# A gated Mamba2 layer with a small expert network on one Trainium2 core: the expert stage in another order

## Chip, core and metric

The kernel runs on one NeuronCore of one Trainium2 chip. The metric is device time in microseconds (us) of one execution. The kernel before takes 1638.48 us, the median of 3 runs (1638.3 to 1638.57).

## What is computed

The input is x, 1024 tokens (4 sequences of 256) of 512 channels in float32. Everything works on its layer norm xn, and the result is `x + s * silu(e)`, where s is a Mamba2 layer and e a small mixture of experts:

```
proj = xn @ in_proj_w.T                       # gate 8192, x 8192, B and C 8 x 128 each, dt 128
xBC  = silu(causal convolution of 4 taps)
dt   = clip(softplus(dt + dt_bias), 0.001, 100)
y    = chunked scan (chunks of 128, 128 heads of 64) + x * D
s    = grouped RMS norm(y * silu(gate)) * norm_w @ out_proj_w.T

probs     = softmax(xn @ gate_w.T)            # 16 experts
vals, idx = top_k(probs, 2);  vals /= sum(vals)
w[token, idx] = vals                          # 0 elsewhere
h = silu(xn @ g.T) * (xn @ u.T)               # 16 experts x 56 channels = 896
e = sum over experts of (h * w) @ d
```

## The kernel before

All products keep float32 accuracy by splitting both operands into a high part (rounded to the float32r type) and a low part (the rest). `product` (lines 448 to 451) then issues three matmuls: high x high, high x low of the tokens, low x high of the weights. A **block** (`channels`) is one tile of 128 output channels over 512 tokens: four contraction tiles of three matmuls, 12 in all.

The program has a prelude and then a long loop. The loop goes over 8 groups of 16 heads, in two halves of 512 tokens each, in 8 steps per half. It isn't touched by the change. The **prelude** normalizes and transposes the tokens, computes the experts, the routing and the time steps, and leads into the loop. It takes about the first tenth of the time.

The experts are computed in 14 tiles e = 0 to 13: 7 tiles of 128 of the 896 channels for each half of the tokens. Tile e = (half, f) needs:

- `expert_in(half, f, 0)` and `expert_in(half, f, 1)` on PE, a block each, for gate and up. Its weights come in through 4 slots of `stg` on SP's DMA queue. ACT writes the high part (`split_first`, line 777), and GpSimd (POOL) the low part (`split_lo`, line 1014), which then frees the slot for SP's next load.
- `expert_tanh(e)` on ACT (line 783) and `expert_gated(e)` on DVE (lines 1118 and 1127), which also free the PSUM banks for tile e + 2.
- `expert_weights(half, f)` on PE (lines 522 and 523): two matmuls that copy each token's routing weight to the 128 channels of the tile, into the PSUM bank `tb`. There is one such bank, so tile e + 1 waits until `expert_weighted(e)` on DVE (line 1133) has read it.
- `expert_hi(e)` on ACT and `expert_lo(e)` on DVE: the split of the result, in 7 buffers for a half. `experts_out(half, t)` on PE needs all 7; it is 21 matmuls for each of the 4 token tiles of a half.

The routing runs across engines: `router` (24 matmuls on PE), `router_turn` (transposes, line 482), `router_exponents` and `router_weights` on DVE, and `route` (transposes on PE, line 564). ACT and DVE then split the weights (lines 843 and 1237), and only then can `expert_weights(0, 0)` run. In `router_weights` 16 small instructions (line 1181), two for each of the 8 token tiles, compare the expert numbers 0 to 15 with a token's chosen index and multiply by its weight. The time steps run between them: `steps_in`, `steps_turn` (line 499), a softplus on ACT (lines 833 to 837) and four wide instructions on DVE (lines 1220 to 1232), `cumulate` and `cumulate_turn`.

At the very start DVE computes mean and variance of 8 token tiles (`tile_stats`), POOL raises the variance to the power -0.5 (`deviation`, line 1009), DVE normalizes (line 1106), PE transposes (`turn_tile`, line 466), ACT and DVE split the transposed tile (lines 764 and 1112). Token tiles 0 to 3 are the first half.

Each engine executes its instructions in the order in which they are written in its own section, and waits on semaphores. No scheduler moves anything: the order of the work is the order of these calls.

Of the kernel before, what the change touches and what calls it, by code (L numbers as in the profile page):

```python
# [7 lines left out]
ALU = mybir.AluOpType  # L8
# [5 lines left out]
P = 128  # L14
# [6 lines left out]
NTT = T // P  # L21
# [132 lines left out]
def build(nc, hid, wstream, wdt, cparams, dtb, rw, consts, sel, out):  # L154
    with ExitStack() as ctx:
# [288 lines left out]
        def _(pe):  # L444
# [138 lines left out]
            steps_turn()  # L583
            experts_in(0, 3)
            experts_in(0, 4)
            experts_in(0, 5)
            route()
            expert_in(0, 6, 0)
            expert_weights(0, 0)
            expert_in(0, 6, 1)  # L590
            expert_weights(0, 1)

            for f in range(3):
                expert_in(1, f, 0)
                expert_weights(*divmod(2 * f + 2, NF))
                if f == 1:
                    cumulate_turn()
                expert_in(1, f, 1)
                expert_weights(*divmod(2 * f + 3, NF))
                if f == 0:  # L600
                    cumulate()
            experts_out(0, 0)
            expert_in(1, 3, 0)
            expert_weights(1, 1)
            expert_in(1, 3, 1)
            expert_weights(1, 2)
            experts_out(0, 1)
            experts_in(1, 4)
            expert_weights(1, 3)
            experts_out(0, 2)  # L610
            experts_in(1, 5)
            expert_weights(1, 4)
            experts_out(0, 3)
            experts_in(1, 6)
            expert_weights(1, 5)
            expert_weights(1, 6)
# [113 lines left out]
            for s in range(4, NJ):  # L730
                step(-1, 1, s, False)
                experts_out(1, s - 4)
# [25 lines left out]
        def _(act):  # L758
# [53 lines left out]
            expert_tanh(0)  # L812
            turned(7)
            for p in FSTEP[0]:
# [3 lines left out]
            expert_tanh(1)  # L818
# [3 lines left out]
            for p in FSTEP[1]:  # L822
                split_first(FPOS[p])
# [5 lines left out]
            expert(2)  # L829
            expert(3)  # L830
# [6 lines left out]
            nc.scalar.activation(tmp1, tmp2, ACT.Ln, bias=1.0).then_inc(S["sp_l"], 1)  # L837
            expert(4)
            expert(5)
            act.wait_ge(S["rt_T"], 1)  # L840
            for i in range(2):
                src = (tb[0:NE, :], pr[2][0:NE, :])[i]
                nc.scalar.activation(wT_hi[i], src, ACT.Copy).then_inc(S["rt_hi"], 1)
            expert(6)
            expert_hi(0)
            expert_hi(1)
            expert(7)
            for i in range(3):
# [6 lines left out]
            expert_hi(2)  # L855
            expert_hi(3)
            expert(8)
            expert_hi(4)
            expert_hi(5)
            expert_tanh(9)  # L860
            expert_hi(6)
            for p in FSTEP[9]:
                split_first(FPOS[p])
            out_tanh(0)
            expert(10)
            out_tanh(1)
            expert(11)
            out_tanh(2)
            expert(12)
            for e in range(7, 11):  # L870
                expert_hi(e)
            out_tanh(3)
            expert(13)
            for e in range(11, 14):
                expert_hi(e)
# [126 lines left out]
        def _(pool):  # L1002
# [88 lines left out]
        def _(dve):  # L1091
# [71 lines left out]
            def router_weights():  # L1163
# [15 lines left out]
                for i in range(NTT):  # L1179
# [359 lines left out]
```

## Time and profile before

| | before |
|---|---|
| median of 3 runs | 1638.48 us |
| profiled execution: its own time | 1638.45 us |
| profiled execution: span | 1636.3 us |
| PE busy | 1598.9 us (98%) |
| DVE busy | 1411.6 us (86%) |
| ACT busy | 1198.4 us (73%) |
| POOL busy | 957.9 us (59%) |
| DMA, mean over the span | 132 GB/s |

The span is the time between the first and the last recorded instruction; the profiled execution's own time is 2.15 us longer. The chain of work that ended last is 84% PE, 8% DVE, 3% ACT and 1% POOL. A row of the timeline gives an instruction's start and its length. An "idle before" beside it is the time for which the engine stood still, with the instruction that released it. Matmuls are pipelined and their ends are modelled: in a full stream the starts lie closer together than the lengths.

### The profile page before, as it was taken

The numbers are of one execution on the slowest core, as the hardware profiler recorded it, in microseconds if no ns is written. First come the engines' busy times: TensorE is split into PE (matmuls) and PEld (weight loads), VectorE is DVE, ScalarE is ACT, GpSimd is POOL, SyncE is SP. The second block draws the span as 40 slices with busy tenths as digits, with TensorE's granted clock in tenths as the row PEclk, the third lists the DMA queues.
The fourth block names the chain that finished last, engine by engine and source line by source line (L and its number), as shares of the span: only waits on it lengthen the run. The fifth ranks groups of instructions, "written<-read, shape, count | busy, mean of one in ns | idle before, by whom it ended". The sixth has DMA issues, their size and how long they took to land.

```text
span 1636.3 us, 28479 instructions
## 1 busy us (share of the span) xinstructions
PE 1598.9 (98%) x8484; PEld 1269.6 (78%) x8484; DVE 1411.6 (86%) x1664; ACT 1198.4 (73%) x2305; POOL 957.9 (59%) x593
## 2 busy tenths in 40 slices
PE   7899989999999999999999999999999999999998
PEld 5677867877778777787777777877778778778776
DVE  6553699988998899998898899989898899889987
ACT  3432688778787778878787878778787878778782
POOL 4522266666566556666566656665576655666563
PEclk9999999999999999999999999999999999999999
DMA  4322344434343344433443334443343434334432
GB/s 150 94 98 94 115 143 149 148 106 150 131 145 135 122 148 147 143 112 123 151 156 128 119 131 152 140 131 129 138 158 110 137 130 158 134 114 148 155 129 90
DMA packets 83719, 216.48 MB, mean 132 GB/s; under 512 B 10576, under 2 KB 12880, under 8 KB 83424
## 3 DMA queue, kind: packets, MB, share of 16 engines
q1 hardware_dynamic: 83264, 214.15, 38.9%
q8 instruction: 81, 1.33, 0.3%
q14 instruction: 86, 0.70, 0.1%
q10 hardware_dynamic: 288, 0.30, 0.1%
HBM read 209.43 MB, written 4.98 MB: 131 GB/s over the span
## 4 chain that ended last, share of the span: by engine, by line
PE 84%; DVE 8%; issue 3%; ACT 3%; POOL 1%; DMA 0%; ACTq 0%; DVEq 0%; POOLq 0%; SPq 0%
PE pj L449 15%; PE pj L451 14%; PE pj L450 14%; PE pr L449 8%; PE pr L450 7%; PE pr L451 7%; PE sc L661 7%; PE sc L665 3%; PE tb L650 3%; DVE conv L1309 2%; POOL w_lo L1014 1%; DVE wo_lo L1373 1%; ACT decay L915 1%; PE pr L639 1%; DVE xc L1323 1%
## 5 line engine op out<-in xcount | busy, mean ns | idle before, releaser
L1014 POOL TENSOR_TENSOR w_lo<-stg,w_hi 128x512 fp32r<-128x512 f32 x316 | 496.2, 1571 | 348.7 <-ACT w_hi L889 263.8
L449 PE MATMUL pj<-xT_hi,w_hi 128*128 128x512 f32 x1208 | 479.3, 397 | 15.8 <-POOL w_lo L1014 7.2
L451 PE MATMUL pj<-xT_hi,w_lo 128*128 128x512 f32 x1208 | 472.6, 391 | 0.0
L450 PE MATMUL pj<-xT_lo,w_hi 128*128 128x512 f32 x1208 | 472.4, 391 | 0.0
L1309 DVE SCALAR_TENSOR_TENSOR conv<-pj,par,conv 128x510 f32<-128x510 f32 (+2 forms) x480 | 357.7, 745 | 80.5 <-ACT conv L897 67.1
L915 ACT ACTIVATE decay<-decay,dtg 128x256 f32<-128x256 f32 (+1 forms) x1024 | 379.0, 442 | 0.0
L1048 POOL TENSOR_TENSOR xc<-xc,thg 128x512 f32<-128x512 f32 x128 | 203.1, 1587 | 188.1 <-DVE xc L1360 188.0
L1054 POOL TENSOR_TENSOR sqsum<-sqsum,sq 128x512 f32<-128x512 f32 x112 | 218.1, 1947 | 114.5 <-ACT sq L941 111.0
L449 PEld LDWEIGHTS pj<-xT_hi,w_hi 128*128 128x128 f32 x1208 | 227.8, 189 | 73.2 <-issue 14.2
L451 PEld LDWEIGHTS pj<-xT_hi,w_lo 128*128 128x128 f32 x1208 | 227.9, 189 | 48.5
L450 PEld LDWEIGHTS pj<-xT_lo,w_hi 128*128 128x128 f32 x1208 | 228.1, 189 | 45.4
L1337 DVE TENSOR_TENSOR decay<-decay,gm 128x1536 f32<-128x1536 f32 x128 | 242.0, 1890 | 0.0
L904 ACT ACTIVATE thx<-conv 128x512 f32<-128x512 f32 x160 | 101.2, 633 | 175.9 <-DVE conv L1309 175.9
L449 PE MATMUL pr<-wo_hi,yT_hi 128*128 128x512 f32 x540 | 221.6, 410 | 0.0
L450 PE MATMUL pr<-wo_lo,yT_hi 128*128 128x512 f32 x540 | 211.1, 391 | 0.0
L451 PE MATMUL pr<-wo_hi,yT_lo 128*128 128x512 f32 x540 | 210.3, 389 | 0.0
L1323 DVE SCALAR_TENSOR_TENSOR xc<-thx,conv 128x512 f32<-128x512 f32 x128 | 196.8, 1542 | 0.2
L923 ACT ACTIVATE decay<-decay 128x1536 f32<-128x1536 f32 x128 | 189.2, 1478 | 0.1
L889 ACT ACTIVATE w_hi<-stg 128x512 fp32r<-128x512 f32 x285 | 176.3, 619 | 17.3 <-PE pj L451 14.5
L661 PE MATMUL sc<-decay,xdt 128*64 128x256 f32 x1024 | 160.5, 392 | 0.0
L897 ACT ACTIVATE conv<-pj,par 128x512 f32<-128x512 f32 x160 | 123.4, 771 | 26.4 <-PE pj L451 25.8
L928 ACT ACTIVATE thg<-pj 128x512 f32<-128x512 f32 x128 | 75.2, 588 | 91.1 <-PE pj L451 91.1
(178 smaller groups left out, 1995.0 us busy)
## 6 DMA issues: line engine op xcount, KB each, us to landing
stg<-wstream SPq DMA_DIRECT2D x387, 256.0 KB, 2.7
decay<-cs_scr SPq DMA_DIRECT2D x128, 768.0 KB, 4.3
acc<-hid SPq DMA_DIRECT2D x8, 256.0 KB, 4.8
out<-acc SPq DMA_DIRECT2D x8, 256.0 KB, 2.0
dt_scr<-decay SPq DMA_DIRECT2D x1, 1024.0 KB, 4.9
gate_scr<-part SPq DMA_DIRECT2D x4, 256.0 KB, 2.0
dtg<-dt_scr SPq DMA_DIRECT2D x16, 64.0 KB, 4.2
stg<-hid SPq DMA_DIRECT2D x4, 256.0 KB, 4.9
```

The source lines that it names most:

```text
L449: nc.tensor.matmul(dst, hi_w, hi_x, start=first, stop=False)
L450: nc.tensor.matmul(dst, hi_w, lo_x, start=False, stop=False)
L451: return nc.tensor.matmul(dst, lo_w, hi_x, start=False, stop=last)
L661: nc.tensor.matmul(sc[hd, c0:c0 + 2 * P], xdt[:, j % 2, 2 * b, hd], decay[:, j % NDEC, 2 * h + b, 0:2 * P], start=True, stop=False)
L915: ins = nc.scalar.activation(d, d, ACT.Relu, scale=-1.0, bias=dtg[:, half, 1, 2 * b + late, 2 * n + h:2 * n + h + 1])
L923: nc.scalar.activation(d, d, ACT.Exp, scale=-1.0).then_inc(S["exp"], 1)
L1014: nc.gpsimd.tensor_tensor(w_dest(n, 1), stg[:, s % RING, :], f32(w_dest(n, 0)), ALU.subtract).then_inc(S["wl"], 1)
L1048: nc.gpsimd.tensor_tensor(xc[:, j, :], xc[:, j, :], thg[:, j % 2, :], ALU.mult).then_inc(S["yg"], 1)
L1054: nc.gpsimd.tensor_tensor(sqsum[:, :], sqsum[:, :], sq[:, :], ALU.add).then_inc(S["sa"], 1)
L1309: nc.vector.scalar_tensor_tensor(out=y[:, :, n:], in0=x[:, :, 0:256 - n], scalar=par[:, 5 * m + 3 - n:5 * m + 4 - n], in1=y[:, :, n:], op0 ...
L1323: nc.vector.scalar_tensor_tensor(out=dst, in0=thx[:, m % 2, :], scalar=1.0, in1=conv[:, m % 2, :], op0=ALU.add, op1=ALU.mult).then_inc(S[" ...
L1337: nc.vector.tensor_tensor(d, d, gm[:, half].unsqueeze(1).to_broadcast([P, 2, 2, 3 * P]), ALU.mult).then_inc(S["w"], 1)
```

## The change

The change is to the order of calls in the prelude, on four engines, and to the instructions of one computation. SP's section is untouched.

- **POOL**: the deviations of token tiles 4 to 7 come after the low parts of the first four weight tiles, not before and between them.
- **PE**: three blocks run ahead of the transposes of token tiles 4 to 6, where one did. Two more blocks run ahead of the time steps (`steps_in`), and one more ahead of `steps_turn`. `route` runs right after `steps_turn` (it was after tile 5), and `expert_weights(0, 0)` two tiles sooner. From there each tile's weighting follows at every block, and `experts_out(0, t)` stand ahead of tiles (1, 2) to (1, 5). `expert_weights(1, 6)` stands between the first two blocks of the next stage.
- **ACT and DVE**: their calls follow the same order. The split of the routing weights stands ahead of the softplus on ACT, and right behind the two additions of the bias on DVE.
- **`router_weights`**: the 16 compare-and-multiply instructions of 128 x 16 become two comparisons and two multiplications of 128 x 128, over all token tiles at once, with broadcast operands.

```diff
 # PE
-            expert_in(0, 0, 0)
+            expert_in(0, 0, 0)
+            expert_in(0, 0, 1)
+            expert_in(0, 1, 0)
             turn_tile(4)
             turn_tile(5)
             turn_tile(6)
-            expert_in(0, 0, 1)
+            expert_in(0, 1, 1)
             turn_tile(7)
-            expert_in(0, 1, 0)
+            expert_in(0, 2, 0)
             router()
-            expert_in(0, 1, 1)
+            expert_in(0, 2, 1)
             router_turn()
             steps_in()
-            experts_in(0, 2)
+            expert_in(0, 3, 0)
             steps_turn()
-            experts_in(0, 3)
-            experts_in(0, 4)
-            experts_in(0, 5)
             route()
+            expert_in(0, 3, 1)
+            expert_in(0, 4, 0)
+            expert_weights(0, 0)
+            expert_in(0, 4, 1)
+            expert_weights(0, 1)
...
+            expert_in(1, 0, 0)
+            expert_weights(0, 6)
+            cumulate()
+            expert_in(1, 0, 1)
+            expert_in(1, 1, 0)
+            expert_weights(1, 0)
+            cumulate_turn()
+            expert_in(1, 1, 1)
+            for f in range(2, 6):
+                experts_out(0, f - 2)
                 expert_in(1, f, 0)
+                expert_weights(1, f - 1)
                 expert_in(1, f, 1)
+            expert_in(1, 6, 0)
             expert_weights(1, 5)
-            expert_weights(1, 6)
+            expert_in(1, 6, 1)
...
-            for s in range(4, NJ):
+            channel_block(-1, 1, ("x", 0))
+            expert_weights(1, 6)
+            channel_block(-1, 1, ("x", 1))
+            experts_out(1, 0)
+            for s in range(5, NJ):
 # ACT
+            expert_tanh(0)
+            for p in FSTEP[0]:
+                split_first(FPOS[p])
+            expert_tanh(1)
             turned(4)
             turned(5)
             turned(6)
...
-            expert(2)
-            expert(3)
+            expert_tanh(3)
+            split_first(FPOS[FSTEP[3][0]])
+            act.wait_ge(S["rt_T"], 1)
+            for i in range(2):
+                src = (tb[0:NE, :], pr[2][0:NE, :])[i]
+                nc.scalar.activation(wT_hi[i], src, ACT.Copy).then_inc(S["rt_hi"], 1)
 # POOL
-            for i in range(5):
+            for i in range(4):
                 deviation(i)
             n = 0
             for s, (kind, half, i) in enumerate(FSEQ):
-                if 1 <= s <= 3:
-                    deviation(4 + s)
+                if s == RING:
+                    for t in range(4, NTT):
+                        deviation(t)
 # DVE, router_weights
-                for i in range(NTT):
-                    for j, dst in enumerate((wr, wr1)):
-                        nc.vector.tensor_scalar(dst[:, i, :], iota, ixf[:, i, j:j + 1], w2[:, i, j:j + 1],
-                                                ALU.is_equal, ALU.mult).then_inc(S["rt_x"], 1)
-                dve.wait_ge(S["rt_x"], 44)
+                for j, dst in enumerate((wr, wr1)):
+                    nc.vector.tensor_tensor(dst, iota.unsqueeze(1).to_broadcast([P, NTT, NE]),
+                                            ixf[:, :, j:j + 1].to_broadcast([P, NTT, NE]), ALU.is_equal
+                                            ).then_inc(S["rt_x"], 1)
+                for j, dst in enumerate((wr, wr1)):
+                    dve.wait_ge(S["rt_x"], 29 + j)
+                    nc.vector.tensor_tensor(dst, dst, w2[:, :, j:j + 1].to_broadcast([P, NTT, NE]), ALU.mult
+                                            ).then_inc(S["rt_x"], 1)
+                dve.wait_ge(S["rt_x"], 32)
                 nc.vector.tensor_tensor(wr, wr, wr1, ALU.add).then_inc(S["rt_s"], 1)
```

**How the order moves, on POOL, at the start.** `mv` is the variance, `w_lo` the low part of a weight tile. Before:

```order
L1009 TENSOR_TENSOR mv<-mv,mhalf 128x1 x5
L1014 TENSOR_TENSOR w_lo<-stg,w_hi 128x512
L1009 TENSOR_TENSOR mv<-mv,mhalf 128x1
L1014 TENSOR_TENSOR w_lo<-stg,w_hi 128x512
L1009 TENSOR_TENSOR mv<-mv,mhalf 128x1
L1014 TENSOR_TENSOR w_lo<-stg,w_hi 128x512
L1009 TENSOR_TENSOR mv<-mv,mhalf 128x1
L1014 TENSOR_TENSOR w_lo<-stg,w_hi 128x512 x3
```

Now:

```order
L1012 TENSOR_TENSOR mv<-mv,mhalf 128x1 x4
L1017 TENSOR_TENSOR w_lo<-stg,w_hi 128x512 x4
L1012 TENSOR_TENSOR mv<-mv,mhalf 128x1 x4
L1017 TENSOR_TENSOR w_lo<-stg,w_hi 128x512 x2
L1029 TENSOR_TENSOR wo_lo<-stg,wo_hi 128x512
```

The first low part no longer stands behind the fifth deviation, and the last four deviations stand behind four low parts.

**How the order moves, on DVE, from the routing to the first weighting.** `gm` holds the routing's small tensors, `decay` the time steps, `wo_hi` and `wo_lo` here the low parts of the routing weights, `xc` the experts' results. Before:

```order
L1175 TENSOR_TENSOR gm<-gm 128x16
L1181 TENSOR_SCALAR gm<-gm 128x16 x16
L1184 TENSOR_TENSOR gm<-gm 128x128
L1220 TENSOR_TENSOR decay<-pr,part 128x512
L1220 TENSOR_TENSOR decay<-sc,part 128x512
L1118 SCALAR_TENSOR_TENSOR thx<-thx,pr 128x512
L1127 TENSOR_TENSOR xc<-thx,pr 128x512
L1118 SCALAR_TENSOR_TENSOR thx<-thx,pj 128x512
L1127 TENSOR_TENSOR xc<-thx,pj 128x512
L1227 SCALAR_TENSOR_TENSOR decay<-decay 128x1024
L1230 TENSOR_SCALAR decay<-decay 128x1024
L1232 TENSOR_TENSOR decay<-decay,part 128x1024
```

Now:

```order
L1179 TENSOR_TENSOR gm<-gm 128x16
L1184 TENSOR_TENSOR gm<-gm 128x128 x2
L1189 TENSOR_TENSOR gm<-gm 128x128 x2
L1192 TENSOR_TENSOR gm<-gm 128x128
L1228 TENSOR_TENSOR decay<-pr,part 128x512
L1228 TENSOR_TENSOR decay<-sc,part 128x512
L1233 TENSOR_TENSOR wo_hi<-tb,yT_hi 16x512
L1233 TENSOR_TENSOR wo_lo<-pr,yT_lo 16x512
L1122 SCALAR_TENSOR_TENSOR thx<-thx,pr 128x512
L1131 TENSOR_TENSOR xc<-thx,pr 128x512
L1137 SCALAR_TENSOR_TENSOR xc<-xc,tb 128x512
```

Sixteen rows became four, and the split of the routing weights (now line 1233) with the first weighting (now line 1137) stand ahead of the wide time-step instructions, which before stood ahead of it.

**How the order moves, on PE, at `route`.** `pr<-cst,conv` and `sc<-cst,conv` are `steps_turn`, `cst,gm` is `route`. Before, the 72 matmuls of tiles 3 to 5 stood between the two; now:

```order
L499 MATMUL pr<-cst,conv 128x128 x4
L499 MATMUL sc<-cst,conv 128x128 x4
L564 MATMUL tb<-cst,gm 16x128 x4
L564 MATMUL pr<-cst,gm 16x128 x4
L449 MATMUL pr<-xT_hi,w_hi 128x512
L450 MATMUL pr<-xT_lo,w_hi 128x512
L451 MATMUL pr<-xT_hi,w_lo 128x512
```

`route` now follows `steps_turn` with nothing between.

## Rows read from the trace of the kernel before

**Rows 1.** Windows: length, busy us (instructions) by engine, granted clock, DMA share, GB/s.

```profile
82.00:83.00 1.00, 1.00 (x3) 0.79 (x3) 0.00 (x0) 0.00 (x0) 0.00 (x0) 0.50 0.02 8
...
170.10:250.00 79.90, 71.73 (x368) 55.99 (x367) 65.90 (x75) 64.16 (x126) 35.97 (x24) 1.00 0.36 121
250.00:1600.00 1350.00, 1346.35 (x7313) 1075.43 (x7314) 1226.74 (x1375) 1067.88 (x2069) 846.34 (x508) 1.00 0.41 137
```

**Rows 2.** Timeline of PE in the prelude: start, length, instruction, [idle before, releaser].

```profile
16.24 0.80 PE L449 MATMUL pj<-xT_hi,w_hi 128*128 128x512 f32 x1 [4.33 <-POOL w_lo L1014]
22.24 0.60 PE L466 MATMUL sc<-cst,acc 128*128 128x128 f32 x4
37.49 0.67 PE L482 MATMUL tb<-cst,xc 16*128 16x16 f32 x8
49.54 0.60 PE L499 MATMUL sc<-cst,conv 128*128 128x128 f32 x4
62.05 0.47 PE L449 MATMUL pr<-xT_hi,w_hi 128*128 128x512 f32 x1 [1.00 <-DVE thx L1118]
69.69 0.50 PE L449 MATMUL pj<-xT_hi,w_hi 128*128 128x512 f32 x1 [1.05 <-POOL w_lo L1014]
72.09 0.39 PE L450 MATMUL pj<-xT_lo,w_hi 128*128 128x512 f32 x1
72.32 0.39 PE L451 MATMUL pj<-xT_hi,w_lo 128*128 128x512 f32 x1
77.50 0.79 PE L522 MATMUL tb<-yT_hi,selr 16*128 16x512 f32 x1 [4.79 <-DVE wo_lo L1237]
83.85 0.50 PE L522 MATMUL tb<-yT_hi,selr 16*128 16x512 f32 x1
102.63 0.49 PE L522 MATMUL tb<-yT_hi,selr 16*128 16x512 f32 x1
106.22 0.49 PE L522 MATMUL tb<-yT_hi,selr 16*128 16x512 f32 x1
156.44 0.49 PE L522 MATMUL tb<-yT_lo,selr 16*128 16x512 f32 x1 [0.78 <-DVE xc L1133]
```

**Rows 3.** Timeline of POOL: a deviation, and the low part of a weight tile.

```profile
9.30 0.78 POOL L1009 TENSOR_TENSOR mv<-mv,mhalf 128x1 f32<-128x1 f32 x1 [0.69 <-DVE mv L1102]
51.31 1.29 POOL L1025 TENSOR_TENSOR wo_lo<-stg,wo_hi 128x512 fp32r<-128x512 f32 x1
```

**Rows 4.** Timeline of DVE: start of the kernel, routing, and a weighting in the middle.

```profile
10.20 0.54 DVE L1106 TENSOR_SCALAR acc<-acc,mv 128x512 f32<-128x512 f32 x1
12.65 0.69 DVE L1112 TENSOR_TENSOR xT_lo<-pr,xT_hi 128x512 fp32r<-128x512 f32 x1 [0.44 <-ACT xT_hi L764]
15.27 1.20 DVE L1106 TENSOR_SCALAR acc<-acc,mv 128x512 f32<-128x512 f32 x1
49.98 0.70 DVE L1166 MAX8 gm<-gm 128x8 f32<-128x16 f32 x8
51.89 0.74 DVE L1170 TENSOR_TENSOR gm<-gm 128x8 f32<-128x8 f32 x1
53.29 6.49 DVE L1181 TENSOR_SCALAR gm<-gm 128x16 f32<-128x16 f32 x16
59.82 0.29 DVE L1184 TENSOR_TENSOR gm<-gm 128x128 f32<-128x128 f32 x1
98.96 0.69 DVE L1133 SCALAR_TENSOR_TENSOR xc<-xc,tb 128x512 f32<-128x512 f32 x1 [1.55 <-PE tb L523]
100.77 0.68 DVE L1138 TENSOR_TENSOR yT_lo<-xc,yT_hi 128x512 fp32r<-128x512 f32 x1
```

**Rows 5.** Timeline of ACT: the routing's exponents, the softplus and the tanh behind it.

```profile
39.79 0.31 ACT L825 ACTIVATE gm<-gm 128x128 f32<-128x128 f32 x1 [0.98 <-DVE gm L1160]
61.34 1.06 ACT L833 ACTIVATE decay<-decay 128x1024 f32<-128x1024 f32 x1 [4.48 <-DVE decay L1220]
67.17 0.60 ACT L783 ACTIVATE thx<-pj 128x512 f32<-128x512 f32 x1
```

More of the change, by code:

```diff
@@ L811, in _ @@
             turned(6)
-            expert_tanh(0)
+            split_first(FPOS[FSTEP[1][0]])
             turned(7)
-            for p in FSTEP[0]:
+            for p in FSTEP[1][1:]:
                 split_first(FPOS[p])
@@ L821, in _ @@
                 nc.scalar.activation(logit_rows[:, i, :], (ob, pr[2])[i][0:NE, :], ACT.Copy).then_inc(S["rt_c"], 1)
-            for p in FSTEP[1]:
+            for p in FSTEP[2][1:]:
                 split_first(FPOS[p])
@@ L837, in _ @@
             nc.scalar.activation(tmp1, tmp2, ACT.Ln, bias=1.0).then_inc(S["sp_l"], 1)
+            for p in FSTEP[3][1:]:
+                split_first(FPOS[p])
             expert(4)
[L839 to L844, printed above, removed]
             expert_hi(0)
             expert_hi(1)
+            expert(5)
+            expert_hi(2)
+            expert(6)
+            expert_hi(3)
+            expert_hi(4)
             expert(7)
+            expert_hi(5)
             for i in range(3):
@@ L854, in _ @@
                 nc.scalar.activation(dst, src, ACT.Copy).then_inc(S["cs_c"], 1)
-            expert_hi(2)
-            expert_hi(3)
+            expert_hi(6)
             expert(8)
[L858 to L870, printed above, removed]
+            for e in range(9, 13):
+                out_tanh(e - 9)
+                expert(e)
+            for e in range(7, 12):
                 expert_hi(e)
-            out_tanh(3)
             expert(13)
-            for e in range(11, 14):
-                expert_hi(e)
+            expert_hi(12)
+            expert_hi(13)
             def split(g, half, s, i):
@@ L1222, in _ @@
                                         dtb_t.unsqueeze(1).to_broadcast([P, 4, NH]), ALU.add).then_inc(S["z"], 1)
+            dve.wait_ge(S["rt_hi"], 2)
+            for i in range(2):
+                nc.vector.tensor_tensor(wT_lo[i], (tb[0:NE, :], pr[2][0:NE, :])[i], f32(wT_hi[i]), ALU.subtract
+                                        ).then_inc(S["rt_lo"], 1)
             expert_gated(3)
+            expert_weighted(0)
             expert_gated(4)
+            expert_weighted(1)
             dve.wait_ge(S["sp_l"], 1)
@@ L1233, in _ @@
                                     a_t.unsqueeze(1).to_broadcast([P, NTT, NH]), ALU.mult).then_inc(S["dtv"], 1)
-            expert_gated(5)
-            dve.wait_ge(S["rt_hi"], 2)
-            for i in range(2):
-                nc.vector.tensor_tensor(wT_lo[i], (tb[0:NE, :], pr[2][0:NE, :])[i], f32(wT_hi[i]), ALU.subtract
-                                        ).then_inc(S["rt_lo"], 1)
-            expert_weighted(0)
-            expert_gated(6)
-            expert_weighted(1)
-            expert_lo(0)
-            expert_weighted(2)
-            expert_lo(1)
-            expert_gated(7)
-            expert_weighted(3)
+            expert_weighted(4)
+            expert_lo(0)
+            expert_gated(6)
+            expert_weighted(5)
+            for e in range(1, 4):
+                expert_lo(e)
+            expert_weighted(6)
             for i in range(2):
```

78 lines of the change are left out of this document (28 added, 50 removed).

## The prediction

> **What bounds the kernel now.** I first read the busy times of the page: PE is busy for 98% of the span, so only time in which PE stands still or runs slowly can be won. Then the windows: in the main part of the loop PE is busy for 1346.35 of 1350 us, with DVE busy for 1226.74 [rows 1]. The change doesn't touch the loop, and there is nothing to win in it. In the stretch from 170.10 to 250 PE has 8.2 us of idle time, in which it waits for DVE; that stretch comes after the change and has the same order. What is left is the prelude, read in PE's timeline [rows 2]. It shows, after the unavoidable start:
>
> - 4.33 us of idle time before the first block, at 16.24, which waited for POOL;
> - 1.00 us at 62.05, which waited for DVE behind the routing comparisons;
> - 1.05 us at 69.69, which waited for a low part on POOL that was late since ACT had been in the softplus;
> - 4.79 us at 77.50, the first weighting, which waited for the split of the routing weights on DVE;
> - 0.78 us at 156.44, two weightings in a row with one bank between them.
>
> There is one more loss. After the long wait the granted clock is 0.50, so 1.2 GHz instead of 2.4 [rows 1]. From 77.50 to 83.85 PE needs 6.35 us for a weighting and a block, for which it needs 3.59 us (102.63 to 106.22) later on [rows 2].
>
> **The start.** POOL's fourth deviation ends at 9.30 + 0.78 = 10.08 [rows 3]. Until now its first low part stood behind the fifth, whose token tile DVE reads late. Now four low parts follow at once, each about 1.3 us, and the first is there at 11.4. The block then waits for the other condition, the low part of token tile 3 on DVE, which ended at 12.65 + 0.69 = 13.34 [rows 4]. That would start the block at 13.4. But the low parts now run beside DVE's normalization of token tile 3 at 10.20, which took 0.54 us with POOL idle. Beside a low part the same instruction took 1.20 us (15.27) [rows 4]. Tile 3's normalization is followed by its transposes, the copy on ACT and the low part, so about 0.9 us of delay arrive at the block. I take 14.3 instead of 16.24, a gain of **1.95 us**. The bounds are 0 (the delay eats all) and 2.8.
>
> The Trainium skill ("SBUF — State Buffer", "Who interferes with whom") says that a DVE instruction in a two-port mode or with two SBUF inputs and a GpSimd instruction that reads SBUF exclude each other for a whole instruction. By that rule the normalization ends just after POOL's low part, which gives the same 14.3. Without it the sum below would be 0.9 us better.
>
> The last four deviations end later than the low parts, at about 20. Their transposes are due only after three blocks, at about 26, so this costs nothing.
>
> **The routing.** `route` follows `steps_turn`, which started near 49.5 [rows 2]. One more block (2.9 us) stands before it, and everything is 1.95 us earlier: `route` is due at about 50.8. Is DVE ready? `router_turn` was at 37.49 [rows 2]; with two more blocks before it and the earlier start it comes at about 41.0 to 41.3. From it to the end of the exponents 2.6 us passed (to 39.79 + 0.31) [rows 2, 5]. From the second row of maxima to the comparisons 3.3 us passed (49.98 to 53.29) [rows 4]. The comparisons then were 6.49 us and are now four instructions of 128 x 128; the one of that size in the trace takes 0.29 us (59.82) [rows 4], and with the last sum that makes 1.5 us. So the weights are there at 41.3 + 2.6 + 3.3 + 1.5 = 48.7, about 2 us before PE wants them. With the sixteen old instructions it would be 53.7, and PE would wait for 2.9 us. So the new form is needed for the new place. The bounds of the four are 0.17 us each (the smallest instructions) and 0.29 plus a whole low part, 1.6 us each.
>
> **Behind `route`.** `route` itself is given 0.8 us. Its two copies on ACT, at most the 0.60 us of a 128 x 512 instruction each (67.17) [rows 5], end at 52.7, DVE's split at about 54. `expert_weights(0, 0)` stands two blocks behind `route`, at 57.3. The wait of 4.79 us goes, with 3 us to spare, and with it the reason for the low clock.
>
> **What is late next.** The softplus on ACT with what belongs to it takes 5.8 us (61.34 to 67.17) [rows 5]. It now starts at 52.7 and delays the tanh of tile 4 to about 59.6. DVE's two steps for tile 4 and the weighting of tile 1 follow, to about 62.3. PE asks for it after one more weighting and block, at about 64.5, so 2.2 us later. From there every weighting has a block of 2.9 us before it and DVE needs 0.7 us for its answer. The wide time-step instructions now stand one at a time between the weightings. The two narrowest places are:
>
> - `experts_out(0, 0)`, which needs all seven low parts. The last follows the weighting of tile 7 and the copies behind `cumulate_turn`. The same sequence stands in the trace: weighting at 98.96, low part done at 100.77 + 0.68 = 101.45, PE at the end of the block behind it at 102.6 [rows 2, 4]. That leaves 1.2 us.
> - `experts_out(1, 0)`: 3.59 us of PE for a weighting and a block, with the last weighting at its head, against 0.69 + 0.60 + 0.68 us for the weighting, ACT's copy and DVE's low part, and some 0.8 us for the hand-overs between them. That leaves 0.8 us.
>
> **The sum.** Matmul ends are modelled: at 72.09 and 72.32 they follow each other at 0.23 us, but a length is 0.39 [rows 2]. So each wait is 0.16 us longer than printed. The four waits after the start are 1.16 + 1.21 + 4.95 + 0.94 = **8.26 us**. The low clock gives 6.35 - 3.59 = **2.76 us**. With the start's 1.95 us that is 12.97 us. The last two weightings, no longer back to back, each interrupt the stream of blocks, and some small new wait is likely at one of the narrow places; I give 0.4 us for both. Saved: 12.6 us. It all lies on PE before the loop, and the loop only starts earlier. The profiled execution's own time is 1638.45 us, 0.03 under the median of the runs, so no correction: 1638.45 - 12.6 = **1625.8 us**.
>
> **Rivals.**
>
> 1. *The narrow places give way.* A low part on DVE waits for a whole low part of POOL, 1.3 us, at both `experts_out`, or the comparisons do. The small sum at 51.89 took 0.74 us and ended with POOL's instruction (51.31 + 1.29) [rows 3, 4]. If two or three such waits land on the path, 2 to 4 us are given back: 1628 to 1630. Against it: POOL has nothing to do for most of the time in which the comparisons now run. By the same rule of the Trainium skill the four comparisons, with two SBUF inputs each, can be held up where the old ones were too.
> 2. *The clock rises sooner.* The first block at 16.24 runs at the low level, and the products are fast again only at about 22.24 (a set of transposes in 0.60 us, as at 49.54) [rows 2]. With the shorter wait before the first block, it may rise earlier relative to the block: up to 2.5 us more, so 1623.3.
> 3. *Slower than before: the loop starts in a worse order.* Before the loop DVE now has some 1 us less lead over PE. In the stretch from 170 to 250 DVE sets the pace, and PE loses 8.2 us there in seven steps [rows 1]. If that pattern went on into the loop, at 0.8 us or more in each of its 16 halves, it would cost 13 us and more and end at about 1640. It decides from 0.8 us a half on. Against it: in the loop DVE is busy for only 91% of the time, and it makes good a late start within a step or two. The loop of before also starts from a stretch in which DVE was behind.
> 4. *No change:* the start gains nothing, and the wait of 4.79 us returns at another place with its low clock, for instance at `route`. That leaves about 2 to 3 us: 1636.
>
> **Chances.** The forecast (1624.5 to 1627.5) has 0.70, rival 1 0.14, rival 2 0.09, rival 3 0.03, rival 4 0.04. The range takes in the forecast, rival 1, and most of rival 2: 1623 to 1630. A difference under 0.2%, 3.3 us, is about what a measurement of this kernel can't tell from none. Faster 0.93, same 0.04, slower 0.03.
>
> **What would show it.** In PE's timeline of the changed kernel the first block starts at 14.3 (13.4 to 14.5), and normalization of token tile 3 takes about 1.2 us or more. There is no idle time over 0.5 us on PE between the first block and 165. The granted clock stays at 1.00 from 25 to 165. The routing's last sum on DVE ends 1 to 3 us before `route`. The loop's stretch starts 12 to 13 us earlier, and the distance from there to the end is unchanged to 0.5 us. I would be wrong if that distance grew, if PE waits at `route` or `experts_out`, or if the low clock is found again behind the first blocks.

## The result, and the profile after

| | before | changed |
|---|---|---|
| median on the same chip, 4 runs each | 1638.53 us (1638.3 to 1638.65) | 1624.81 us (1624.04 to 1625.73) |
| profiled execution: its own time / span | 1638.45 / 1636.3 us | 1624.73 / 1622.6 us |
| PE busy | 1598.9 us (98%) | 1594.7 us (98%) |
| DVE busy | 1411.6 us (86%) | 1409.1 us (87%) |
| ACT / POOL busy | 1198.4 / 957.9 us | 1197.7 / 957.5 us |
| start of the loop's stretch (`bc`) | 170.14 | 155.66 |
| from there to the end of the span | 1466.16 us | 1466.94 us |

The ratio is 0.9917, with a 95% interval of 0.9899 to 0.9934: the changed kernel is 0.8% faster. The forecast was 1625.8 us, in a range of 1623 to 1630. The windows of the changed kernel (length, busy us and instructions of PE, PEld, DVE, ACT, POOL, granted clock, DMA share, GB/s) answer to [rows 1]:

```profile
24.00:160.00 136.00, 136.00 (x618) 104.07 (x617) 74.62 (x135) 54.16 (x92) 50.45 (x36) 1.00 0.34 108
160.00:250.00 90.00, 81.49 (x433) 63.50 (x432) 77.06 (x85) 74.58 (x147) 43.32 (x29) 1.00 0.37 120
250.00:1600.00 1350.00, 1346.25 (x7309) 1074.80 (x7308) 1223.12 (x1375) 1059.55 (x2051) 843.84 (x507) 1.00 0.41 136
```

PE is busy for all of the 136 us from 24 to 160, and the clock is never granted lower there. The loop is as full as it was. These are all of PE's waits from 0 to 170 (line, what it waited for, total us, times, longest):

```profile
PE tb L466 <- DVE acc L1110: 6.6, 1, 6.6
PE pj L449 <- POOL w_lo L1017: 1.5, 1, 1.5
PE pr L466 <- DVE acc L1110: 1.2, 2, 0.8
PE sc L466 <- DVE acc L1110: 0.3, 1, 0.3
```

Of the five waits of [rows 2] only the one before the first block is left, with 1.51 instead of 4.33 us (the other rows are waits for the first transposes, ahead of that block; new among them are the 0.8 us before token tile 3's, at 11.35, which are the price of the overlap). PE's timeline, to be set against [rows 2]:

```profile
13.97 0.77 PE L449 MATMUL pj<-xT_hi,w_hi 128*128 128x512 f32 x1 [1.51 <-POOL w_lo L1017]
16.66 0.57 PE L449 MATMUL pj<-xT_hi,w_hi 128*128 128x512 f32 x1
17.08 0.40 PE L450 MATMUL pj<-xT_lo,w_hi 128*128 128x512 f32 x1
17.31 0.40 PE L451 MATMUL pj<-xT_hi,w_lo 128*128 128x512 f32 x1
...
49.12 0.60 PE L564 MATMUL tb<-cst,gm 128*16 128x128 f32 x4
...
55.56 0.49 PE L522 MATMUL tb<-yT_hi,selr 16*128 16x512 f32 x1
...
59.15 0.49 PE L522 MATMUL tb<-yT_hi,selr 16*128 16x512 f32 x1
...
62.73 0.49 PE L522 MATMUL tb<-yT_hi,selr 16*128 16x512 f32 x1
...
91.30 0.39 PE L449 MATMUL sc<-wo_hi,yT_hi 128*128 128x512 f32 x1
...
148.18 0.39 PE L449 MATMUL sc<-wo_hi,yT_hi 128*128 128x512 f32 x1
...
155.66 0.59 PE L638 MATMUL pr<-bc 128*128 128x256 f32 x2
```

The first products follow each other at 0.43 us, and from 17.08 on at 0.23 us. That is near the ratio of the two clock levels, but the granted clock doesn't show it here:

```profile
16.00:17.00 1.00, 1.00 (x4) 0.81 (x3) 0.97 (x3) 0.00 (x0) 0.69 (x1) 1.00 0.36 113
```

It reads 1.00 while the products stand 0.43 us apart, the distance that they have at a granted 0.50 later on (79.24 to 83.08 in the kernel before). So at the kernel's start this text calls "the low level" what the steps show, and that it is the clock is inferred from them. The weightings follow at 3.59 us from the first one on. DVE's timeline answers to [rows 4]:

```profile
9.88 1.40 DVE L1110 TENSOR_SCALAR acc<-acc,mv 128x512 f32<-128x512 f32 x1
...
13.13 0.69 DVE L1116 TENSOR_TENSOR xT_lo<-pr,xT_hi 128x512 fp32r<-128x512 f32 x1 [0.64 <-ACT xT_hi L767]
...
44.31 0.50 DVE L1184 TENSOR_TENSOR gm<-gm 128x128 f32<-128x128 f32 x2
44.72 0.49 DVE L1189 TENSOR_TENSOR gm<-gm 128x128 f32<-128x128 f32 x2
45.25 0.29 DVE L1192 TENSOR_TENSOR gm<-gm 128x128 f32<-128x128 f32 x1
...
51.90 0.67 DVE L1233 TENSOR_TENSOR wo_lo<-pr,yT_lo 16x512 fp32r<-16x512 f32 x1
...
59.98 0.68 DVE L1137 SCALAR_TENSOR_TENSOR xc<-xc,tb 128x512 f32<-128x512 f32 x1
...
89.53 0.68 DVE L1142 TENSOR_TENSOR yT_lo<-xc,yT_hi 128x512 fp32r<-128x512 f32 x1
...
147.16 0.69 DVE L1142 TENSOR_TENSOR yT_lo<-xc,yT_hi 128x512 fp32r<-128x512 f32 x1 [0.70 <-ACT yT_hi L792]
```

And POOL's answers to [rows 3], with the low parts that now follow the fourth deviation:

```profile
8.99 0.78 POOL L1012 TENSOR_TENSOR mv<-mv,mhalf 128x1 f32<-128x1 f32 x1 [0.69 <-DVE mv L1106]
9.74 2.68 POOL L1017 TENSOR_TENSOR w_lo<-stg,w_hi 128x512 fp32r<-128x512 f32 x2
```

The row of the first block names POOL as its releaser, but the block asks only for the first low part, and that was written at about 11.1. What it waited for is the low part of token tile 3 on DVE, which ended at 13.13 + 0.69 = 13.82. A second profile of the same kernel (e9) names DVE there, after the same wait of 1.50 us.

**Where the 14.48 us before the loop came from.** The first block starts 2.27 us sooner. The four later waits were worth 8.26 us, the low clock behind the longest 2.76. The products also turned fast sooner relative to the first block: the 12 matmuls of that block took 4.26 us (13.97 to 18.23) instead of 5.28 (16.24 to 21.52), and the first transposes behind it, which in the kernel before still ran in part at the low level, 0.3 us less. These terms make 14.6 us. The rest of the program took 0.78 us more. Read at the first step of each half, the shift between the two traces goes up and down between 13.7 and 14.5 us; it is 14.5 at the first half and 13.7 at the last.

### The profile page after: what moved, and what is told of

Its sections match the earlier page's. It is cut to its first block, busy times and chain, and to the rows that moved or that the text cites. A ratio compares the mean times of both kernels' runs of the same rounds, so it can differ in the third digit from the quotient of the medians.

```text
span 1622.6 us, 28467 instructions
## 1 busy us (share of the span) xinstructions
PE 1594.7 (98%) x8484; PEld 1266.8 (78%) x8484; DVE 1409.1 (87%) x1652; ACT 1197.7 (74%) x2305; POOL 957.5 (59%) x593
## 4 chain that ended last, share of the span: by engine, by line
PE 89%; DVE 6%; ACT 2%; issue 2%; POOL 1%; DMA 0%; SPq 0%; ACTq 0%; DVEq 0%; POOLq 0%
PE pj L449 16%; PE pj L451 15%; PE pj L450 15%; PE pr L449 9%; PE pr L450 8%; PE pr L451 8%; PE sc L660 7%; PE sc L664 3%; PE tb L649 3%; DVE conv L1310 2%; PE pr L638 1%; DVE wo_lo L1374 1%; PE tb L673 1%; ACT decay L918 1%; DVE xc L1324 1%
```

## The experiments

One number comes back in nearly all of them, so here is a table first. "First block" is its start; "fast after" is the distance from there to the first product that stands less than 0.30 us behind the one before it; "loop" is the start of the loop's stretch; "way" is the distance from the first block to it. In before and e2 three groups of transposes stand behind the first block, and the second of them is already fast, at 22.24 and 22.91; there the slow stretch ended at most 6.1 us after the block's start, sooner than the column says. The times are medians. The kernels before on the same chips had 1638.56 us (first four), 1639.3 (next four) and 1639.05 (last four).

| kernel | first block | fast after | loop | way | median us (runs) | ratio, 95% interval |
|---|---|---|---|---|---|---|
| before | 16.24 | 7.34 | 170.14 | 153.90 | | |
| changed | 13.97 | 3.34 | 155.66 | 141.69 | 1624.81 (4) | 0.9917 [0.9899, 0.9934] |
| e1_before_pool | 14.24 | 3.32 | 167.79 | 153.55 | 1637.03 (11) | 0.9986 [0.9977, 0.9995] |
| e2_before_cmp | 16.83 | 7.41 | 166.66 | 149.83 | 1633.54 (5) | 0.9966 [0.9952, 0.9979] |
| e3_after_oldcmp | 13.87 | 6.31 | 156.98 | 143.11 | 1626.17 (5) | 0.9920 [0.9907, 0.9934] |
| e4_after_oldpool | 16.44 | 3.37 | 158.14 | 141.70 | 1626.13 (5) | 0.9921 [0.9907, 0.9934] |
| e5_order_only | 17.73 | 4.27 | 159.91 | 142.18 | 1627.04 (5) | 0.9923 [0.9909, 0.9936] |
| e6_before_fill | 15.88 | 3.02 | 165.31 | 149.43 | 1636.30 (8) | 0.9978 [0.9968, 0.9989] |
| e7_after_warm | 13.97 | 3.70 | 155.76 | 141.79 | 1624.54 (4) | 0.9910 [0.9895, 0.9926] |
| e8_after_warm_more | 13.90 | 0.76 | 154.39 | 140.49 | 1622.87 (4) | 0.9895 [0.9880, 0.9911] |
| e9_after_again | 14.08 | 6.28 | 157.14 | 143.06 | 1624.75 (4) | 0.9908 [0.9892, 0.9923] |
| e10_after_poolwait | 13.43 | 5.54 | 156.24 | 142.81 | 1624.52 (4) | 0.9911 [0.9896, 0.9926] |
| e11_best | 13.83 | 0.53 | 154.08 | 140.25 | 1623.99 (4) | 0.9904 [0.9889, 0.9919] |
| e12_before_x0 | 15.92 | 4.12 | 167.62 | 151.70 | 1637.55 (11) | 0.9990 [0.9981, 0.9999] |

### e1: POOL's new order alone

```diff
 # the kernel before, POOL
-            for i in range(5):
+            for i in range(4):
                 deviation(i)
...
-                if 1 <= s <= 3:
-                    deviation(4 + s)
+                if s == RING:
+                    for t in range(4, NTT):
+                        deviation(t)
```

> The kernel before with POOL's new order alone (four low parts ahead of the last four deviations). Theory, each part of the change pays by the waits it takes off PE: the first block starts at about 14.0 instead of 16.24, the normalization of token tile 3 takes about 1.4 us beside POOL's low part instead of 0.54, and all else is as before, so 2.3 us are saved, and up to 1.3 us more if the products turn fast sooner after the first block's start, as they did in the changed kernel: 1635 to 1636.4 us. Rival, the early start is eaten by the next thing in line (the transposes of token tiles 4 to 6, which here stand after a single block while their deviations now come last): PE waits there for 1 to 2 us, and under 1.5 us are saved.

The start gained 2.0 us (14.24 against 16.24), with 6.86 against 6.91 for the first transposes. The normalization took 1.40 us, and all later waits stood as they were. The transposes of tiles 4 to 6, which in this kernel come after one block, were late by 0.2 us only, so the rival fell by the trace. The median is 1.5 us lower, 0.6 us short of the range that I expected. The profile holds a surprise, in the windows behind the 0.78 us wait between the last two weightings, which now starts its weighting at 152.47:

```profile
152.00:153.00 1.00, 0.53 (x2) 0.29 (x2) 0.41 (x1) 0.55 (x1) 0.00 (x0) 1.00 0.96 332
153.00:154.00 1.00, 1.00 (x4) 0.72 (x4) 0.77 (x2) 0.12 (x2) 0.00 (x0) 0.90 1.01 322
154.00:157.00 3.00, 3.00 (x8) 2.30 (x7) 1.73 (x3) 0.59 (x1) 0.00 (x0) 0.50 0.85 304
```

The granted clock falls to 0.50 for some 3.3 us, which the kernel before doesn't show at that place ([rows 2] has the same wait at 156.44). At 0.43 instead of 0.23 us for a product that costs 1.5 us, and it is why the way of e1 is only 0.35 us shorter than before's in spite of the sooner rise at the start and of 0.76 us less at the low clock behind the long wait (5.59 us for the stretch that takes 6.35 in [rows 2]).

### e2: the wide comparisons alone

```diff
 # the kernel before, DVE
-                for i in range(NTT):
-                    for j, dst in enumerate((wr, wr1)):
-                        nc.vector.tensor_scalar(dst[:, i, :], iota, ixf[:, i, j:j + 1], w2[:, i, j:j + 1],
-                                                ALU.is_equal, ALU.mult).then_inc(S["rt_x"], 1)
+                for j, dst in enumerate((wr, wr1)):
+                    nc.vector.tensor_tensor(dst, iota.unsqueeze(1).to_broadcast([P, NTT, NE]),
+                                            ixf[:, :, j:j + 1].to_broadcast([P, NTT, NE]), ALU.is_equal
+                                            ).then_inc(S["rt_x"], 1)
...
```

> The kernel before with the four wide comparisons alone, in the old order. Theory: DVE is done with the routing some 5 us sooner (54.5 instead of 60.1), so the wait of 1.00 us at 62.05 goes, the softplus on ACT starts some 5 us sooner, and with it the wait of 1.05 us at 69.69. route still stands behind tile 5, and its split on DVE behind the wide time-step instructions, so of the 4.79 us a part stays: saved 2 us and as much of the long wait as the earlier softplus frees, 3 to 7 us in all. [...] Rival, the order alone held the first weighting back: the long wait stays at over 4 us and only 2 us are saved.

PE's waits from 0 to 170:

```profile
PE pj L449 <- POOL w_lo L1014: 5.2, 1, 5.2
PE tb L522 <- DVE wo_lo L1241: 2.8, 1, 2.8
PE tb L522 <- DVE xc L1133: 0.8, 1, 0.8
```

The waits of 1.00 and 1.05 us are gone and the long one is down by 2.0 us, so in the old order the wide comparisons are worth some 4 us of way, and the median fell by 5.0 us. The rival fell too. PE's timeline behind the shorter wait:

```profile
73.60 0.49 PE L522 MATMUL tb<-yT_hi,selr 16*128 16x512 f32 x1 [2.84 <-DVE wo_lo L1241]
...
74.40 0.79 PE L449 MATMUL pj<-xT_hi,w_hi 128*128 128x512 f32 x1
...
78.76 0.50 PE L522 MATMUL tb<-yT_hi,selr 16*128 16x512 f32 x1
```

From one weighting to the next it is 5.16 us, not 3.59: this shorter wait of 2.84 us was also followed by the low clock (granted 0.50 from 75 to 77), which set in after PE had resumed and cost 1.57 us. And, as in e1, it came back behind the 0.78 us wait (at 151.37): seven products from 152.6 to 155.6 stand 0.43 us apart.

### e3: the changed kernel with the sixteen old comparisons

The edit of e2 in reverse, in the changed kernel.

> The changed kernel with the sixteen old comparisons in the new order. Theory: DVE's weights are ready 5.3 us later than in the changed kernel (45.5 there, now about 50.8), and route was due on PE at 49.12, so PE waits 1.5 to 2 us at route and nothing else changes, since the wait is too short for the clock to fall: 1.5 to 2.5 us slower than the changed kernel. Rival, the comparisons carry most of the gain: the delay is passed on to the softplus, the weightings and experts_out, and 4 us or more are lost.

The comparisons on DVE, and `route` on PE:

```profile
45.64 3.28 DVE L1185 TENSOR_SCALAR gm<-gm 128x16 f32<-128x16 f32 x16
48.95 0.29 DVE L1188 TENSOR_TENSOR gm<-gm 128x128 f32<-128x128 f32 x1
```

```profile
50.44 0.60 PE L564 MATMUL tb<-cst,gm 128*16 128x128 f32 x4
```

**This expectation fell.** The sixteen instructions take 3.28 us, half of the 6.49 of [rows 4], and the weights are there 1.2 us before `route`. PE waits for nothing between the first block and 170 in this kernel either. e5, with the same sixteen in the new order, has 3.27 us for them. In the trace before, POOL wrote three low parts while the sixteen ran (54.12 to 55.43 and 56.41 to 58.95, 3.9 us), and single ones of them took up to 1.38 us. Here POOL's last low part ends at 44.09 and its next starts at 50.96. The loop starts 1.3 us later than in the changed kernel, but only since the clock rose 3.0 us later: e9, the changed kernel itself, shows the same way (143.06 against 143.11) with the same rise. The median is 1.4 us above the changed kernel's, and the intervals of the two ratios overlap: the times don't contradict the trace, and don't confirm it either.

### e4 and e5: the old order on POOL, and the order of calls alone

e4 is the changed kernel with e1's edit in reverse; e5 has the edits of e3 and e4 together.

> The changed kernel with POOL's old order. Theory: the first block starts at 16.2 again, and everything behind it keeps its distance: 2.3 us slower than the changed kernel, and up to 1.3 us more if the products again turn fast only some 6 us after the first block's start. Rival, the clock depends on time since the kernel's start and not on the first block's: the products turn fast at the same time as in the changed kernel (17.0), and 1.1 to 1.3 us are won back, so that it is only 1 us slower.

> The changed kernel with POOL's old order and the sixteen old comparisons, so the order of the calls alone. Theory after the first four runs: where POOL is idle the old comparisons take 3.3 us, and their weights are ready at route in the new order, so they cost nothing there; POOL's old order costs 2.3 us at the start. All four later waits and the low clock are gone: the loop's stretch starts 12 us earlier than in the kernel before (near 158), the whole 1626 to 1627 us, the same as with the new comparisons and POOL's old order. Rival, the comparisons pay as soon as POOL's low parts fall beside them, since the first block starts later here: a wait of 1 us or more at route, 1628 us.

In e4 the first block waits for 4.80 us and starts at 16.44; the way is 141.70 us, as in the changed kernel (141.69). So POOL's order is worth what the first block gains and nothing behind it. The products turn fast at 19.81, not at 17, and 3.37 us after the first block, as in the changed kernel, so the rival fell. The median is 1.3 us above the changed kernel's, where 2.3 was expected. In e5 the load of the third token tile landed late (DVE waited for it for 1.03 us, up to 7.42), which led to a wait of 1.41 us on PE at 9.03 and moved the first block to 17.73. Behind it there is no wait. The order of calls alone shortens the way by 11.7 us (153.90 to 142.18, the sooner rise among it) and the median by 12.3 us. The other two parts together add 1 to 2.5 us by the ratios, which the intervals of the ratios don't separate from nothing.

### e6: PE kept busy through the long wait

```diff
 # the kernel before, PE
             expert_in(0, 6, 0)
+            pe.wait_ge(S["z"], 2)
+            for i in range(20):
+                nc.tensor.matmul(sc[:, :], xT_hi[:, 0, 0:P], xT_hi[:, 0, 0:H], start=True, stop=True)
             expert_weights(0, 0)
```

> The kernel before with 20 extra matmuls of 512 columns into a PSUM bank that is free at that time, put ahead of the first weighting, so inside the wait of 4.79 us; their product isn't used. Theory, what PE loses behind that wait is the low clock: the matmuls fill 4.6 us of the wait, the granted clock stays at 1.00, the stretch from the first weighting to the second falls from 6.35 to 3.6 us, and the loop's stretch starts 2.7 us earlier. Rival, the block behind the wait is slow for another reason (its weights or its PSUM bank): it stays at 5 us or more, and nothing is saved.

```profile
70.80 4.70 PE L591 MATMUL sc<-xT_hi 128*128 128x512 f32 x20
75.46 0.49 PE L522 MATMUL tb<-yT_hi,selr 16*128 16x512 f32 x1
...
79.04 0.49 PE L522 MATMUL tb<-yT_hi,selr 16*128 16x512 f32 x1
```

With PE busy up to the weighting, weighting and block take 3.58 us instead of 6.35. The granted clock stays at 1.00. The low clock is a consequence of the idle time, and in the trace of before it costs 2.77 us. How much it costs varies: behind nearly the same wait (4.68 and 4.66 us) the same stretch took 5.59 us in e1 and 5.87 in e12, so 2.0 and 2.3 us. The median fell by 3.0 us. The loop starts 4.8 us sooner in this profile; 1.4 us of that is the sooner rise at the start, which isn't due to the edit.

### e7, e8 and e9: the clock at the start

e7 puts 11 matmuls on zeros ahead of the first transposes (DVE writes the zeros first, with a memset that isn't shown below); e8 puts 4 more behind them; e9 is the changed kernel again.

```diff
 # the changed kernel, PE; e7
+            pe.wait_ge(S["warm"], 1)
+            for i in range(11):
+                nc.tensor.matmul(pr[0][:, :], yT_lo[:, 0, 0:P], yT_lo[:, 0, :], start=True, stop=True)
             pe.wait_ge(S["consts"], 16)
             for i in range(4):
                 turn_tile(i)
 # e8, as well
+            for i in range(4):
+                nc.tensor.matmul(pr[0][:, :], yT_lo[:, 0, 0:P], yT_lo[:, 0, :], start=True, stop=True)
             expert_in(0, 0, 0)
```

> The changed kernel with 11 extra matmuls on a zeroed tile at the very start, while PE waits for the first token tile; their product isn't used. Theory, PE's first blocks run at the low level until PE has worked for some 3 to 7 us: with PE at work from about 1.5 us on, the products are fast from the first block on (steps of 0.23 us), which saves 1.4 to 3 us of the 3 to 6 us that ran slowly. Rival, the clock falls back between 6 and 14 us, when PE mostly waits for DVE: the first block starts slowly as before and nothing is saved.

> As the run before it, with four more such matmuls behind the transposes of token tile 3, in the wait ahead of the first block. Theory: they end before the block's data is there, so they cost nothing, and where the clock fell back in the run before, it may be held up here: 1.4 to 3 us better than the changed kernel. Rival: at the low level they take 1.7 us and push the first block back by up to 0.3 us.

> The changed kernel once more, unchanged, beside the next three on the same chip. Every theory: 13 to 15 us under the kernel before. Where the products turn fast should lie anywhere from 3 to 7 us behind the first block's start, as in the runs so far, and move the time by up to 2 us with all else equal.

PE in e7:

```profile
2.49 4.90 PE L570 MATMUL pr<-yT_lo 128*128 128x512 f32 x11 [2.49 <-DVE yT_lo L1102]
7.23 0.60 PE L466 MATMUL tb<-cst,acc 128*128 128x128 f32 x4
...
11.43 0.66 PE L466 MATMUL pr<-cst,acc 128*128 128x128 f32 x4 [1.26 <-DVE acc L1114]
13.97 0.77 PE L449 MATMUL pj<-xT_hi,w_hi 128*128 128x512 f32 x1 [1.89 <-POOL w_lo L1020]
14.54 0.63 PE L450 MATMUL pj<-xT_lo,w_hi 128*128 128x512 f32 x1
```

The transposes run at the high level (0.60 us for four instead of 1.08). By the first block, behind gaps of 0.2 to 1.9 us, the level is low again (0.43 us from product to product), and nothing is gained: the rival came true. In e8:

```profile
12.05 2.05 PE L575 MATMUL pr<-yT_lo 128*128 128x512 f32 x4
13.90 0.70 PE L449 MATMUL pj<-xT_hi,w_hi 128*128 128x512 f32 x1
14.43 0.39 PE L450 MATMUL pj<-xT_lo,w_hi 128*128 128x512 f32 x1
14.66 0.39 PE L451 MATMUL pj<-xT_hi,w_lo 128*128 128x512 f32 x1
```

Here the products are fast from the second one on, as in e11, and the way is 1.2 us shorter than in the changed kernel's profile. The level wasn't held up all the way: the transposes at 11.28 took 1.11 us, and the four matmuls behind them 2.05 us (1.18 in e11, where the level stayed high), so it had fallen and rose again by 14. e9 brings the opposite: the same kernel as the changed one was fast only 6.28 us after its first block, and its loop started 1.48 us later. A slow product loses 0.20 of its 0.43 us, and 0.47 of the 2.94 us by which the rise came later is 1.37 us, exactly the difference of the ways (143.06 against 141.69).

### e10 and e11: POOL's first low part after the fourth normalization

```diff
 # the changed kernel, POOL
             for i in range(4):
                 deviation(i)
+            pool.wait_ge(S["xn"], 4)
             n = 0
```

> The changed kernel, in which POOL's first low part waits until token tile 3 is normalized. Theory: the normalization goes back from 1.40 us to 0.54, its transposes and copies come 0.6 to 0.9 us sooner, the first low part is there at 11.8 and still ahead of the token tile's low part; the first block starts at about 13.3 instead of 13.97, and the loop 0.7 us sooner. Rival, something else had set the start (the fourth weight tile's copy on ACT, or the load of the third): the first block stays at 13.8 or later.

> The wait of the run before and the 15 extra matmuls of the warm-up together. Theory: the two add up, 0.7 us and 1.3 to 3 us: the loop's stretch starts at 153.3 to 153.8 (155.66 in the changed kernel), the whole 2 to 3 us under the changed kernel. Rival, with the earlier block the four matmuls stand in its way: 1 us or more of the gain is lost.

DVE, then PE, in e10:

```profile
10.15 0.54 DVE L1111 TENSOR_SCALAR acc<-acc,mv 128x512 f32<-128x512 f32 x1
```

```profile
6.86 1.09 PE L466 MATMUL tb<-cst,acc 128*128 128x128 f32 x4 [6.86 <-DVE acc L1111]
...
13.43 0.76 PE L449 MATMUL pj<-xT_hi,w_hi 128*128 128x512 f32 x1 [1.57 <-DVE xT_lo L1117]
```

The normalization takes 0.54 us again, and the first block starts 6.57 us after the first transposes, against 7.38 in the changed kernel: the overlap costs 0.8 us, and the rival fell. In the times this can't be told from nothing. e11 has the edits of e8 and e10 together. It didn't add up: ACT's copy for the fourth transposes stood behind the split of the third weight tile, whose load was late, so the block started at 13.83. It has the earliest loop (154.08) and a median between e8's and the changed kernel's.

### e12: a block between the last two weightings, in the kernel before

```diff
 # the kernel before, PE
             expert_weights(1, 5)
-            expert_weights(1, 6)
...
-            for s in range(4, NJ):
+            channel_block(-1, 1, ("x", 0))
+            expert_weights(1, 6)
+            channel_block(-1, 1, ("x", 1))
+            experts_out(1, 0)
+            for s in range(5, NJ):
                 step(-1, 1, s, False)
                 experts_out(1, s - 4)
```

> The kernel before with a block between the last two weightings. Theory: the wait of 0.78 us at 156.44 goes, and the interrupted stream costs 0.15 us: the loop's stretch starts 0.8 us sooner, in the times hardly to be seen. Rival, experts_out(1, 0) now waits for the last low part of DVE, since there is one block less between: nothing is saved.

The 0.78 us wait is gone, the weightings stand 3.59 us apart (153.03 and 156.62), and the median is 1.5 us lower, with an interval that just leaves out no change. From the block that follows the transposes of tile 6 the loop is 1.2 us nearer than before (145.89 against 147.11), more than the 0.94 us of the wait, but 0.5 us of it is a shorter stretch at the low clock behind the long wait (5.87 against 6.35 us), which isn't due to the edit. That leaves 0.7 us, about the 0.8 expected, and the rival fell: no wait stands at `experts_out`.

**What beats both.** The best median is e8's, 1622.87 us. Its four runs lie at 1621.94 to 1624.02, the eight of the changed kernel and of e9 at 1624.02 to 1625.73. That is some 1.9 us, but the intervals of the ratios (0.9880 to 0.9911 and 0.9892 to 0.9923) overlap. I call it likely, not settled. From e7 to e11 the loop starts between 154.1 and 157.1, so little is left to win before it.

## Why the prediction was right, point by point

- **The bound.** PE in the prelude, and only there: right. The windows of the loop are the same before and after, and the way to the loop took all of the gain.
- **The start, 1.95 us.** Measured 2.27, of which 0.32 is luck: the load of the second token tile, behind which DVE normalizes the first, landed sooner, and the first transposes start at 6.59 against 6.91. From the first transposes to the block it is 1.95 us less. The price of the overlap was right too: the normalization takes 1.40 us, ends at 11.28, 0.2 us behind POOL's first low part (9.74 + half of 2.68 = 11.08), and e10 shows 0.54 without it. By the rule of the Trainium skill ("SBUF — State Buffer", "Who interferes with whom"), that a DVE instruction in a two-port mode and a GpSimd instruction wait for each other whole, the trace agrees; in which mode the normalization ran no row tells.
- **The four waits, 8.26 us, and the low clock, 2.76 us.** Right: none of them is left, and none has taken their place. e6 measured the low clock by itself, at 2.77 us. That the sum could take it at 2.76 is the case of this one profile of before: over e1, e2 and e12 it came to 2.0, 1.6 and 2.3 us.
- **The routing.** Ready at 45.5, forecast 48.7; `route` at 49.12, forecast 50.8; the split of the weights done at 52.57, forecast 54; the first weighting at 55.56, forecast 57.3. I had spent too much on the way from `router_turn`, since durations came from a stretch where POOL ran beside DVE: the small sum took 0.74 us there and takes 0.15 here. **The step that failed** is "With the sixteen old instructions it would be 53.7, and PE would wait for 2.9 us. So the new form is needed for the new place." Its term of 6.49 us was half contention. e3 measured 3.28 us and no wait: the weights were ready 1.2 us before `route`. My own text had the reason at hand: against rival 1 it says that POOL has nothing to do in the stretch where the comparisons now run. It would have been right for the sixteen too. The total wasn't touched, since the sum credited the waits and not the instructions.
- **What is late next.** The weighting of tile 1 ends on DVE at 60.66, and PE asks for the next at 62.73: 2.1 us, forecast 2.2. `experts_out(0, 0)`: the last low part ends at 90.21, PE comes at 91.30, 1.1 us, forecast 1.2. `experts_out(1, 0)`: 147.85 against 148.18, 0.3 us, forecast 0.8. Both held, the second barely.
- **The rivals.** The narrow places didn't give way. No order in the loop was worse than before: the distance from its start to the end grew by 0.78 us, more than the 0.5 I had named as a test, so one of my own signs of being wrong came up. But it lies between 1465.3 and 1469.0 us over all 14 profiles, whatever was edited, so the test was too sharp to mean anything. No wait came back at `route`. Rival 2, the clock that rises sooner, came true by half: 1.3 us. e9 shows that it isn't a property of the change, since the same kernel rose 2.9 us later, and the kernels with the old order rose after 3.0 to 6.1 us as well.
- **The total.** The saving was 13.7 us, forecast 12.6, and part of the closeness is terms that cancel: the rise at the start gave 1.3 us and the start 0.3 us that the sum didn't have, the 0.4 us set aside for interruptions came to 0.1, and the loop's 0.8 us went the other way.
- **What carries the gain.** The order of calls: 12.3 us in e5's median. The wide comparisons are worth 5.0 us in the old order, and nothing that these runs can separate in the new one. The two are no sum: both remove the same waits.

I didn't foresee one benefit. The last two weightings stand back to back in four profiles (before, e1, e2, e6). In two of them, e1 and e2, the wait of 0.78 us was followed by a stretch at the low clock that cost 1.5 us. The changed order has no such wait, and in none of the nine profiles with it do products run at the low level after 22 us.

## What to carry to other kernels

Add up PE's waits from the trace, and with each of them the low clock that the trace shows behind it; a new order that removes them is then worth their sum, if every new due time is checked against the readiness of its producer. Take the duration of small DVE instructions from a stretch in which POOL is idle before saying that a shorter form is needed: here sixteen of them took 6.49 us beside POOL and 3.28 without. And where the gain is about ten us, a second profile of the same kernel tells how much of a difference is the clock's rise at the start.

## What the runs showed of the hardware

- The time from the first block to the fast products was 3.0 to 6.3 us in the kernels without warm-up, and 3.34 and 6.28 in two profiles of the same kernel. The granted clock reads 1.00 throughout, so it has to be read from the steps of the products (0.43 and 0.23 us). The Trainium skill ("TensorE: Matmul & The Clock Gate", "Part 1: The HAM clock gate") says that the number of slow matmuls at the start of one kernel varies from run to run. These two profiles agree, at 7 and 14 slow ones.
- The granted clock fell behind a wait of 2.84 us (e2), and in e1 and e2 behind one of 0.78 us between weightings, but not in before and e6, which have the same wait. What decides it there, these runs don't tell. In before it fell some 4 us into the wait (0.85 from 76 to 77), in e2 only after PE had resumed.
- The high level was lost again between 12 and 14 us in e7, after four short groups of transposes with gaps between them.
- Sixteen tensor_scalar instructions of 128 x 16 follow each other at 0.2 us (3.28 us for all) with POOL idle, and up to 1.38 us beside a low part on POOL.
